# Output weights summed on VectorE and prepared beside later batches, mask and xT loaded earlier, projection independent of the turned query

## The reference

```
q = layernorm(x) @ Wq + bq;  k = ctx @ Wk + bk;  v = ctx @ Wv + bv        # head of 32
s = q k^T / sqrt(512);  s = (s - mean(s)) / (std(s) + eps), plus a tiny mask term
head = softmax(s) @ v
attention = tile(head, 16) @ Wout + bout
x = x + tanh(g_xattn) * attention
logits = layernorm(x) @ router_w^T;  the 2 best of 8 experts, weights normalised
x = x + tanh(g_ffn) * sum of the 2 chosen experts (silu(x w1) * (x w3)) w2
```

## Time and profile before

| what | value |
|---|---|
| median of 3 timed runs | 420.26 us (420.23 to 421.08) |
| the profiled execution | 421.31 us, span in the trace 419.7 us |
| PE busy | 369.8 us, 88% of the span |
| DVE, ACT, POOL busy | 53%, 45%, 32% |
| chain that ended last, by engine | PE 79%, DMA 10%, issue 3% |
| granted TensorE clock, mean | 0.939 |

### The profile page before, as it was taken

One profiled execution on the slowest core, in us unless ns is written; L12 is line 12 of the kernel. 1 busy time (PEld: TensorE's weight loads), 2 busy tenths in 40 slices (PEclk: granted clock), 3 DMA queues, 4 the chain that ended last, 5 costly groups with the idle time before them and its releaser, 6 DMA issues.

```text
span 419.7 us, 7103 instructions
## 1 busy us (share of the span) xinstructions
PE 369.8 (88%) x1984; PEld 280.2 (67%) x1985; DVE 223.4 (53%) x464; ACT 190.6 (45%) x314; POOL 132.5 (32%) x246
## 2 busy tenths in 40 slices
PE   2979999870199999998999999999999999999990
PEld 2435545530078888886787888888888888888870
DVE  2135886654662765396961229626653962765020
ACT  1123454447603773478552238427634752772120
POOL 2333577665221222313141231413233142231301
PEclk9978999855589999999999999999999999999996
DMA  7986889941294687287983227736872773210201
GB/s 242 354 284 201 301 263 368 300 139 40 63 407 183 165 290 242 50 283 254 391 269 89 50 37 225 267 150 154 286 243 50 266 260 117 50 30 1 50 0 16
DMA packets 17553, 78.00 MB, mean 186 GB/s; under 512 B 3618, under 2 KB 4770, under 8 KB 10372
## 3 DMA queue, kind: packets, MB, share of 16 engines
q1 hardware_dynamic: 11060, 66.79, 45.5%
q0 software_dynamic: 4720, 7.78, 9.4%
q10 hardware_dynamic: 1760, 3.28, 2.3%
HBM read 71.20 MB, written 7.54 MB: 188 GB/s over the span
## 4 chain that ended last, share of the span: by engine, by line
PE 79%; DMA 10%; issue 3%; DVE 2%; ACT 2%; POOL 2%; POOLq 1%; ACTq 0%; DVEq 0%
PE turnA L442 20%; PE turnB L442 20%; PE scp L462 20%; PE kvp L307 5%; DMA xn_d<-xn 4%; PE kvp L449 3%; DMA xg<-xn_d,gidx 3%; PE scp L429 2%; DMA ent_next<-lists_d 2%; PE turnA L293 2%; PE turnA L360 1%; PE turnA L344 1%; PE scp L332 1%; PE turnB L318 1%; PE turnA L367 1%
## 5 line engine op out<-in xcount | busy, mean ns | idle before, releaser
L774 DVE TENSOR_TENSOR w13l<-stage,w13h 128x1024 fp32r<-128x1024 f32 x64 | 75.8, 1220 | 8.5 <-DMA lists_d<-entry,place 4.7
L569 ACT ACTIVATE w13h<-stage 128x1024 fp32r<-128x1024 f32 x64 | 64.5, 1053 | 0.2
L442 PE MATMUL turnA<-w13h,xTh 128*128 128x512 f32 x128 | 51.5, 402 | 1.7 <-DVE xTl L857 1.7
L442 PE MATMUL turnB<-w13h,xTh 128*128 128x512 f32 x128 | 51.9, 405 | 0.0
L462 PE MATMUL scp<-w2h,hTh 128*128 128x512 f32 x128 | 51.7, 404 | 0.0
L442 PE MATMUL turnA<-w13h,xTl 128*128 128x512 f32 x128 | 51.2, 400 | 0.0
L442 PE MATMUL turnA<-w13l,xTh 128*128 128x512 f32 x128 | 51.1, 399 | 0.0
L442 PE MATMUL turnB<-w13l,xTh 128*128 128x512 f32 x128 | 50.5, 395 | 0.0
L442 PE MATMUL turnB<-w13h,xTl 128*128 128x512 f32 x128 | 50.5, 395 | 0.0
L462 PE MATMUL scp<-w2l,hTh 128*128 128x512 f32 x128 | 50.2, 392 | 0.0
L462 PE MATMUL scp<-w2h,hTl 128*128 128x512 f32 x128 | 49.8, 389 | 0.0
(11 more groups left out here) (162 smaller groups left out, 611.9 us busy)
## 6 DMA issues: line engine op xcount, KB each, us to landing
stage<-in_w_dram SPq DMA_DIRECT2D x48, 1024.0 KB, 4.9
ctx_t<-in_ctx_dram SPq DMA_DIRECT2D x8, 1444.0 KB, 12.4
x_t<-in_x_dram SPq DMA_DIRECT2D x8, 200.0 KB
xT_t<-in_xT_dram SPq DMA_DIRECT2D x8, 200.0 KB, 6.9
out_dram<-x ACTq DMA_DIRECT2D x8, 200.0 KB
xn_d<-xn ACTq DMA_DIRECT2D x8, 200.0 KB
stage<-in_wout_dram SPq DMA_DIRECT2D x1, 1024.0 KB, 11.4
ent_next<-lists_d POOLq DMA_DIRECT2D x17, 1.0 KB, 2.0
```

What stands on the lines that cost most here:

```text
L442: mm = pe.matmul(region, xp[:, c, :], wp[:, q, c, :], start=(c == 0 and i == 0), stop=(c == HC - 1 and i == 2))
L569: act.activation(dst, src, ACT.Copy).then_inc(S["w_hi"], 1)
L774: dve.tensor_tensor(lo, raw, hi.bitcast(F32), ALU.subtract).then_inc(S["w_lo"], 1)
```

## The change

- VectorE sums Wout's four row chunks in three additions (`add_wout`, start of round 1); TensorE then needs one matmul with a wider `sel` (128x128) and one with a single row for bout (`brow`), in round 1. ScalarE scales the result straight into `wsum`. `wraw` is gone.
- The transposing of `wsum` comes at the end of round 1, its product with the router weights (`route_weights`) in round 2. `outputs(0)` moves from the end of round 1 to round 2, behind `query(3)`; VectorE's copy to `wx9` and `raw_logits(0)` stand at the start of its round 2.
- Loads: xT(0) ahead of x(0), mask ahead of context 0, context 1 ahead of bout and Wout, and bout once.
- `project` waits for the context alone; `turn_values` takes over the wait for the turned query copy. `turn_query(b)` waits for `make_values(b-1)`.
- `vP` lies in the second bank of `kvp`, so its waits on x2, and that of `outputs` on the values, go. `query` waits for `lg_made` from batch 4 on only. The zero fill by GpSimd is awaited in `turn_values(0)` instead of before the first query. The exp of the mask stands at the end of ScalarE's round -1.

```
-        vP = turnA[:, 0:KT * D]
+        vP = kvp[:, 512:512 + KT * D]
...
+            load_xT(0)
             load_x(0)
-            load_xT(0)
+            sp.dma_start(mask_u[:], mask).then_inc(S["mask_in"], 16)
             load_ctx(0)
-            sp.dma_start(mask_u[:], mask).then_inc(S["mask_in"], 16)
             load_x(1)
             load_xT(1)
+            load_ctx(1)
+            sp.dma_start(bout_r[:], bout.rearrange("(o d) -> o d", o=1)).then_inc(S["bout_in"], 16)
             sp.dma_start(stage2[:, 0:HC, :], Wout.rearrange("(c p) n -> p c n", p=P)).then_inc(S["wout_in"], 16)
-            sp.wait_ge(S["wraw_zero"], 1)
-            for r in range(2):
-                sp.dma_start(wraw[VW * r + D:VW * r + D + 1, :], bout.rearrange("(o d) -> o d", o=1)).then_inc(S["bout_in"], 16)
-            load_ctx(1)
             load_x(2)
...
             def turn_query(b):
                 pe.wait_ge(S["q_fixed"], 2 * (b + 1))
+                if b >= 1:
+                    pe.wait_ge(S["v_made"], b)
                 pe.transpose(qTp, qn[:], ident[0:SQ, 0:SQ]).then_inc(S["q_turned"], 1)
...
             def project(b):
                 pe.wait_ge(*ring("ctx_in", NC, b))
-                pe.wait_ge(S["qT_copied"], b + 1)
...
             def turn_values(b):
+                pe.wait_ge(S["qT_copied"], b + 1)
                 pe.wait_ge(S["kv_copied"], b + 1)
-                if b >= 2:
-                    pe.wait_ge(S["x2_ready"], b - 1)
+                if b == 0:
+                    pe.wait_ge(S["zero_made"], 1)
...
             def sum_weights():
-                pe.wait_ge(S["wout_in"], 16)
-                pe.wait_ge(S["v_made"], 1)
-                for c in range(HC):
-                    for r in range(2):
-                        mm = pe.matmul(outp[r * VW:r * VW + D, :], sel[:], stage2[:, c, :], start=(c == 0), stop=(c == HC - 1))
-                mm.then_inc(S["wsum_done"], 1)
+                pe.wait_ge(S["wout_added"], 3)
+                pe.wait_ge(S["bout_in"], 16)
+                pe.wait_ge(S["brow_made"], 3)
+                pe.matmul(outp, sel[:], stage2[:, HC, :], start=True, stop=False)
+                pe.matmul(outp, brow[:], bout_r[:], start=False, stop=True).then_inc(S["wsum_done"], 1)
...
             for i in ROUNDS:
                 if live(i):
                     project(i)
+                if i == 2:
+                    route_weights()
                 if live(i - 1):
                     turn_prob(i - 1)
+                if i == 2:
+                    pe.wait_ge(S["wx9_made"], 1)
                 if live(i + 1):
                     query(i + 1)
+                if i == 2:
+                    outputs(0)
                 if live(i):
                     turn_values(i)
                     scores(i)
+                if i == 1:
+                    sum_weights()
                 if live(i - 1):
                     heads(i - 1)
                 if live(i + 1):
                     turn_query(i + 1)
-                if i == 0:
-                    sum_weights()
+                if i == 1:
+                    turn_weights()
                 if live(i - 2):
                     ranks(i - 2)
-                if live(i - 1):
+                if live(i - 1) and i != 1:
                     outputs(i - 1)
...
+            def add_wout():
+                dve.wait_ge(S["wout_in"], 16)
+                for j in range(2):
+                    dve.tensor_tensor(stage2[:, HC + j, :], stage2[:, 2 * j, :], stage2[:, 2 * j + 1, :], ALU.add).then_inc(S["wout_added"], 1)
+                dve.wait_ge(S["wout_added"], 2)
+                dve.tensor_tensor(stage2[:, HC, :], stage2[:, HC, :], stage2[:, HC + 1, :], ALU.add).then_inc(S["wout_added"], 1)
...
             for i in ROUNDS:
+                if i == 2:
+                    copy_low_weights()
+                    raw_logits(0)
                 if live(i - 2):
                     choose(i - 2)
                     add_attention(i - 2)
+                if i == 1:
+                    add_wout()
                 if live(i - 3) and i <= NB + 1:
                     make_weights(i - 3)
```

More of the change, by code:

```diff
@@ L112, in gated_block @@
         wqr = sb(a, "wqr", [P, HC, VW + E])
-        wraw = sb(a, "wraw", [P, H])
+        bout_r = sb(a, "bout_r", [1, H])
         wsum = sb(a, "wsum", [P, H])
@@ L117, in gated_block @@
         inv_h = sb(a, "inv_h", [P, P])
-        sel = sb(a, "sel", [P, D])
+        sel = sb(a, "sel", [P, P])
+        brow = sb(a, "brow", [1, P])
         g_t = sb(a, "g_t", [P, 2])
@@ L289, in query @@
                 pe.wait_ge(*ring("xT_in", NT, b))
-                if b >= 3:
+                if b >= 4:
                     pe.wait_ge(S["lg_made"], b - 2)
@@ L362, in sum_weights, with turn_weights, route_weights @@
             def sum_weights():
[L363 to L368 removed]
+                pe.wait_ge(S["wout_added"], 3)
[3 more added lines that the diff above has]
+                pe.matmul(outp, brow[:], bout_r[:], start=False, stop=True).then_inc(S["wsum_done"], 1)
+            def turn_weights():
                 pe.wait_ge(S["wsum_made"], 1)
                 for c in range(HC):
[L371 removed]
+                    mm = pe.transpose(outp[:, c * P:(c + 1) * P], wsum[:, c * P:(c + 1) * P], ident[:])
                 mm.then_inc(S["wsum_turned"], 1)
+            def route_weights():
                 pe.wait_ge(S["wsumT_copied"], 1)
[L374 removed]
+                pe.wait_ge(S["q_fixed"], 6)
+                pe.wait_ge(S["head_copied"], 1)
                 for c in range(HC):
@@ L386, in _ @@
             pe.wait_ge(S["ones_made"], 1)
-            pe.wait_ge(S["sel_made"], 1)
-            pe.wait_ge(S["zero_made"], 1)
+            pe.wait_ge(S["sel_made"], 3)
             pe.wait_ge(S["wqr_made"], 3)
@@ L492, in _, with exp_mask @@
             act.activation(g_t[:], sm[:, O_G:O_G + 2], ACT.Tanh).then_inc(S["tanh_done"], 1)
-            act.wait_ge(S["mask_made"], 1)
-            act.activation(emask[:].rearrange("p b k -> p (b k)"), mask_f[:], ACT.Exp).then_inc(S["emask_made"], 1)
+            def exp_mask():
+                act.wait_ge(S["mask_made"], 1)
+                act.activation(emask[:].rearrange("p b k -> p (b k)"), mask_f[:], ACT.Exp).then_inc(S["emask_made"], 1)
             def softmax_exp(b):
@@ L547, in copy_qT, with scale_weights, copy_turned_weights @@
                 act.activation(qT[b % 2][:], qTp, ACT.Copy, scale=float(H) ** -0.5).then_inc(S["qT_copied"], 1)
-            def wsum_steps():
+            def scale_weights():
                 act.wait_ge(S["wsum_done"], 1)
-                act.wait_ge(S["wraw_zero"], 1)
-                for r in range(2):
-                    act.activation(wraw[r * VW:r * VW + D, :], outp[r * VW:r * VW + D, :], ACT.Copy).then_inc(S["wraw_set"], 1)
+                act.wait_ge(S["tanh_done"], 1)
+                act.activation(wsum[:], outp, ACT.Copy, scale=g_t[:, 0:1]).then_inc(S["wsum_made"], 1)
+            def copy_turned_weights():
                 act.wait_ge(S["wsum_turned"], 1)
-                act.activation(wsumT[:].rearrange("p c s -> p (c s)"), turnB[:, 0:HC * P], ACT.Copy).then_inc(S["wsumT_copied"], 1)
+                act.activation(wsumT[:].rearrange("p c s -> p (c s)"), outp, ACT.Copy).then_inc(S["wsumT_copied"], 1)
             def split_hi(e, unit, last):
@@ L577, in _ @@
                     copy_probT(i - 1)
+                if i == 1:
+                    scale_weights()
+                if live(i - 1):
                     copy_head(i - 1)
@@ L580, in _ @@
                     copy_qT(i + 1)
-                if i == 0:
-                    wsum_steps()
+                if i == -1:
+                    exp_mask()
+                if i == 1:
+                    copy_turned_weights()
                 if live(i - 2):
@@ L664, in _ @@
             dve.wait_ge(S["ident_made"], 1)
-            dve.tensor_reduce(sel[:], ident[:].rearrange("p (j m) -> p m j", m=D), AX.X, ALU.add).then_inc(S["sel_made"], 1)
+            dve.memset(sel[:], 0.0).then_inc(S["sel_made"], 1)
+            dve.wait_ge(S["sel_made"], 1)
+            for r in range(2):
+                dve.tensor_reduce(sel[:, r * VW:r * VW + D], ident[:].rearrange("p (j m) -> p m j", m=D), AX.X, ALU.add
+                                  ).then_inc(S["sel_made"], 1)
+            dve.memset(brow[:], 0.0).then_inc(S["brow_made"], 1)
+            dve.wait_ge(S["brow_made"], 1)
+            for r in range(2):
+                dve.memset(brow[:, r * VW + D:r * VW + D + 1], 1.0).then_inc(S["brow_made"], 1)
             def ln1_stats(b):
```

11 lines of the change are left out of this document (2 added, 9 removed).

## The result

The changed kernel took 428.16 us (median; 426.81 to 430.57) where the kernel before took 420.67 beside it: ratio 1.0152, 95% interval 1.0115 to 1.0188. The sign and the mechanisms were forecast; the size was too small. The forecast was 4.5 us more, 424.8; by the ratio it is 6.4 us more, by the medians 7.5, and the median lies 0.16 us beyond the high end of the range, 428.0. The profiled execution took 428.16 us with a span of 426.2, against 419.7 before: 6.5 us more in the trace.

What follows compares the result with a forecast made beforehand. The attention part's chain of waits was taken to set when the unbroken expert matmuls start. Marker M: 47.3 at full clock plus 2.4, 0.9 and 1.9 for low clock, 52.5, 4.5 us late; 420.26 + 4.5 = 424.8 us, range 419.8 to 428.0.

Steps and rivals of the forecast that it cites:

- R1: Start of turning the probabilities of batch 0 on TensorE; 32.98 us before the change, forecast 27.4.
- The lock: Wout additions on VectorE delay GpSimd's sigma(0), both using SBUF: 1.0 us taken, bounds nothing and 2.06.
- Round 1 at full clock: Work from turning batch 0's probabilities to turning batch 1's, new weight sum included: 9.15 us, before 7.72.
- Round 2 at full clock: From turning batch 1's probabilities to batch 2's: 10.7 us against 7.32, TensorE idling 2.2 ahead of heads(1).
- The clock: Idle TensorE brings half clock: round 1 work 2.4 us more, weight sum 0.9, round 2's projection 3 1.9.
- R2: Start of turning the probabilities of batch 1 on TensorE; 40.70 us before the change.
- The rival in which the fall costs nothing: Round 2's gap does not lower the clock, dropping the 1.9 us: 422.9 us, chance 13%.
- the one in which most of round 2 runs at half clock: Clock falls before heads(1), and late first rise: 3.7 us more, 428.5 us, chance 10%.
- The faster rival: Batch 2's x lands before batch 0's scores end, about 19 us, and TensorE hardly idles: 418.1 us, chance 14%.
- M: Start of turning batch 2's probabilities, after which both kernels run the same rounds; before 48.02 us, forecast 52.5.
- The tail moves as a whole: Batch 7's context, expert weights and batch 3's put hang on M, so its 4.5 us delay reaches the end.
- The rival of the absorbing tail: Transfer backlog sets the 16.11 us store's landing, end hardly moves: 420.3 us, 13%; includes lock and clock away (-0.7 - 1.0 + 1.5).

Runs made afterwards that it cites:

- first gap filled: Changed kernel plus seven dummy matmul calls in round 1, ahead of turning batch 0's probabilities, none in round 2; ratio 1.0008 to the kernel before.
- both fillers: Changed kernel plus dummy matmuls in both TensorE gaps: seven calls in round 1, two ahead of heads(1) in round 2; ratio 0.9974 to the kernel before.
- additions moved: Changed kernel with VectorE's three Wout additions moved behind the statistics of x(3), away from GpSimd's sigma steps of batch 0; ratio 1.0106 to the kernel before.
- control: The changed kernel itself, unaltered, run again on a second chip; 425.88 us, ratio 1.0118 to the kernel before.
- softmax 0 first: Changed kernel with VectorE's score statistics and GpSimd's sigma of batch 0 ahead of batch 2's x statistics and norm; ratio 0.9995 to the kernel before.

## Why the prediction was right or wrong

*What the change removes.* Right: R1 came 6.8 us earlier and not 8.3, for the reason given, x of batch 2 ahead of the scores; turning the order round brought R1 to 21.9. I took 21.41 for its landing "again". It was 20.43, and in other executions of the same queue 18.98, 19.80 and 21.88: a landing read from one trace is good to about 1.5 us. The exp of batch 0 so began at 25.14, ahead of the 26 to 27.5 that I had named. Projection 1 began at 17.1 and not at 19.6: the earlier query, mask and projection did bring the work forward, behind the same wait, and made the idle time 6.4 us instead of 5.4.

*The lock.* Price forecast 1.0 between 0 and 2.06, measured 0.75, confirmed by moving the additions. With x(2) a microsecond early, R1 was 26.15 instead of 27.4.

*Round 1 at full clock.* 9.15 forecast; the kernels with the first gap filled took 9.5 and 9.4.

*Round 2 at full clock.* 10.7 forecast, 10.67 measured in the kernel with both fillers and in the one with the additions moved; the wait ahead of heads(1) 2.2 forecast, 2.24 measured. The sum from single rows, wait included, holds to a tenth.

*The clock.* This is where the sum went wrong: the term for round 1 was too small. For round 1 I put 3.3 us (2.4 on the first 2.46 us of work, 0.9 on the sum), expecting dense matmuls to raise the clock midway through the sum. It stayed low until 38.0, so the sum (+2.1), heads, transposes and part of projection 2 paid as well: 14.8 from R1 to R2 against 9.5 filled, 5.3 us, and in the control 6.6. The step that failed is "dense matmuls are what raised the clock again before": the rise at the end of projection 1 in the trace of before said that dense work ends in a rise, not that less of it is enough. For round 2 I put 1.9; it was 1.6 in the first trace (12.3 against 10.7), 1.6 with the first gap filled, 2.9 in the control, 3.3 with softmax 0 first, and nothing in the kernel with the additions moved. The row that sized this term, 4.45 us at 13.00, stands at a granted clock of 1.00 from 13 to 17 in the trace of before, so the record has no low clock there that it could recover from, and that 1.9 came near is luck. The rival in which the fall costs nothing and the one in which most of round 2 runs at half clock both occurred, behind the same gap.

*The faster rival* wanted x(2) before about 20 and the clock kept. In the kernel with the additions moved x(2) came at 18.98, TensorE still idled 4.84 us ahead of R1, and its clock fell: an earlier x alone does not do it.

*M and the end.* M forecast 52.5, measured 53.3. That is closer than its terms deserve: an R1 that was 1.25 us early, 1.0 of it by the chance of the landing, hid part of the 2.0 us by which the clock term of round 1 was too small. "The tail moves as a whole" was off by 1.2 us. The gidx step alone was 1.04 longer, beside VectorE's splits, of the same kind as the earlier trace rows and absent in the control. That makes 6.5 us in the trace, where 4.5 was forecast. The rival of the absorbing tail was not the main story, but it is not empty: from M to X the traces took between 64.8 and 68.9 us without order, and the put or store that ends last there between 11.7 and 17.1. Which of the transfers queued beside it decides its length was not tried and stays open. The 1.5 us that this rival adds for its last case, with lock and clock both away, has no row behind it; without it that case would be 1.7 us faster than before.

## What to carry to other kernels

Before moving work off TensorE's path, list the waits it was hiding, and price each twice: once as idle time, and once as all the work behind it at half clock until the clock rises again. Here 6.4 us of idle time that had cost nothing by itself (R1 was 6.8 us early all the same) cost 5.3 more in the round behind it (6.6 in the control). An experiment with dummy matmuls in the gap separates the two in one run, and the cure was cheap: let each engine serve the batch that is waiting before the one whose data has yet to land.

## What the runs showed of the hardware

The granted clock does not follow a gap in a fixed way. The same wait of 2.24 to 2.25 us ahead of heads(1) was followed by a fall during the wait (control), 0.8 to 1.9 us behind its end (softmax 0 first, changed, first gap filled), and by none (additions moved: 45.67, with the outputs behind it at 1.08 us). Once at half clock, TensorE stayed there from 24.3 to 38.0 with back-to-back work from 26.15 on, and in the control until 42.1 with such work from 27.6 on, while the second stretch of the changed kernel ended after 3.4 us. What decides between these was not found.

Three dummy calls, of 2.5 us in all where TensorE idled otherwise, made the kernel before slightly faster (0.9966, 0.9936 to 0.9996): projection 1 took 2.63 us instead of 5.04, and M came 3.1 us earlier.

Small GpSimd instructions beside VectorE additions with two SBUF inputs took 0.88 to 0.97 us instead of 0.55. They were held up, though both sides got through in turn: 0.75 us was paid beside 1.9 us of additions. In the kernel with softmax 0 first the same additions lay beside the last step of sigma, and that took 0.81 us instead of 0.27. The Trainium skill, "SBUF — State Buffer" (SBUF: two separate sides), has the loser of this lock blocked for the whole instruction; these rows agree with the lock, and show that in a chain of short instructions it falls on only some of them.
